# Layer 1's shared second pass moved from behind the expert loop into the routing chain

## The chip, the cores and the metric

The kernel runs on one core of one Trainium2 chip. The core has five engines with their own instruction streams: TensorE (PE: matmuls, transposes), VectorE (DVE), ScalarE (ACT), GpSimd (POOL, which here mostly issues indirect DMAs, "gathers") and SyncE (SP, which here issues DMAs only). They run beside one another and wait for each other by semaphores. The metric is the time of one execution on the device, in microseconds (us). A second, profiled execution gives the trace; its span runs from the first to the last instruction.

## The reference

A "macaron" block on 2048 tokens of 256 numbers: half of a feed-forward layer, an attention-like scan, and half of the same feed-forward layer again, with the same weights.

```python
x = x + 0.5 * ffn(layernorm(x))      # layer 0
x = x + attn(layernorm(x))           # W_in, a scan over the tokens, W_out
x = x + 0.5 * ffn(layernorm(x))      # layer 1, the same weights

def ffn(x):
    scores = sigmoid(gate_w @ x) + gate_b
    weights, indices = top_k(scores, 4)           # 4 of 16 experts
    weights = weights / weights.sum(-1)
    shared_out = silu(x @ w1_shared) * (x @ w3_shared) @ w2_shared    # width 176
    routed_out = sum over the 4 experts e of
        weights[e] * (silu((x @ w1[e]) * (x @ w3[e])) @ w2[e])
    return shared_out + routed_out
```

## The kernel before

The tokens lie in 16 tiles of 128 (NT = 16). They stay in SBUF as `xres` [128 x 16 x 256] from the first load to the last store. Everything is float32, and every engine's stream is written out by hand, with explicit semaphores; nothing reorders it. Loops over experts are hardware loops with a few iterations unrolled.

Each of the two feed-forward layers (f = 0 and f = 1) has the same stages:

1. **Phase A.** Each tile is normalized and written to DRAM (`xn_scratch`, for the gathers). PE turns it, and computes the gate logits and the shared expert's first pass (`hidden`, L1380 with `w_shared`). The silu product, the *shared hidden* rows [128 x 176], stays in SBUF (`hidk`, made of leftover room in `stage`, `raw_shared`, `hid_room` and `ring_f`).
2. **Routing chain.** DVE makes the top-4 masks and weights, PE counts the tokens of each expert (`count`, L1524 and L1526), DVE turns the counts into slots (`route_slots`). Each expert gets whole tiles of 128 slots, 79 in all (NS = 79). PE finds the expert of each slot tile (`tile_experts`, L1533). Then come 16 *picks*, one for each token tile: ACT scales rows (`scale_pick`, L770), and PE multiplies (`pick`, L1540). Out of them comes `tokidx`, the token of each slot (cast at L1095).
3. **Expert loop.** For each of the 79 slot tiles POOL gathers 128 rows (L560), PE turns them (L1402; ACT evicts at L664), and runs the expert's two passes (L1380, L1431). ACT evicts the result, and SP writes it to `ys_scratch` (`y_out`, L449). For the first 8 token tiles the finished expert rows are gathered back and added within the loop ("early" rows).
4. **Behind the loop.** POOL gathers the rows of the other 8 token tiles, 4 each, so 32 gathers (`combine`, L595), and DVE multiplies each with its weight and adds it to `xres` (L1159 in layer 1).

The shared expert's **second pass** (the hidden rows times `w2_shared`) stands in different places in the two layers.

In **layer 0** it runs within the routing chain, in 17 *shared steps*. In step n PE turns the hidden rows of tile n (`turn_early`, L1475: two transposes), ACT copies them to SBUF (`copy_early`, L741), PE multiplies those of tile n-1 (`out_early`, L1488: two matmuls), and ACT evicts the sums of tile n-2 with the factor 0.5 (`evict_early`, L748). Step 0 stands ahead of `count`, steps 1 to 11 between `count` and `tile_experts`, the rest among the picks. Between the steps ACT also turns a few late experts' weights into the format of the matmul (`high_expert`, L645 and L648; `CHAIN_HIGHS` says after which step). SP writes the 16 results to DRAM (`shared_scratch`, L457) and loads them again during the loop, four at a time (`shared_in`, L462). DVE adds each to `xres` in the loop (`shared_rows_first`, L1139).

In **layer 1** SP writes the hidden rows to DRAM (`hid_out`, L453) ahead of the loop, and loads them again (`hid_in`, L467): 6 at the loop's start, 8 more behind the loop's last y_out, 2 after that. The rest is done behind the loop, for 8 pairs of tiles: PE turns a pair (`turn_hidden`, L1506), ACT copies it (`copy_hidden`, L762), PE multiplies (`shared_out`, L1517), and DVE adds the sums to `xres` from PSUM (`shared_sum`, L1181). POOL's 32 gathers are paced by this: ahead of every second gather POOL waits for one more step of PE's work (`SHARED_DONE`). An output tile is stored (L522) once its sum is added; the store of the last tile is the last thing in the kernel.

In the rows, `bank` is PSUM, `mamba_room`, `stage`, `raw_ring`, `ring_f` and `ring_r` are SBUF buffers that serve several purposes, `cst` and `hcst` are constants, and `si` holds the slot numbers for the gathers.

Of the kernel before, what the change touches and what calls it, by code (L numbers as in the profile page):

```python
# [31 lines left out]
LAG_HID = 5  # L32
# [16 lines left out]
HID_AHEAD = 6  # L49
SUMS_AFTER = {9: (0, 1), 10: (2,), 11: (3,), 12: (4,), 13: (5,), 14: (6, 7)}  # L50
CHAIN_HIGHS = {1: (6, 7, 8, 9), 5: (10,), 8: (11,)}
# [34 lines left out]
def build(nc, x_d, w13r_d, w2r_d, w13s_d, w2s_d, wm_d, cst_d, hcst_d, out_d):  # L86
# [7 lines left out]
    with ctx:  # L94
# [9 lines left out]
        hid_dram = nc.dram_tensor("shared_hidden", (N, H), f32, kind="Internal").ap()  # L104
# [44 lines left out]
        hTs = [raw_ring[0:HC, b * 512:(b + 1) * 512] for b in range(4)]  # L149
# [48 lines left out]
        hidb = [r0(b * H, (b + 1) * H) for b in range(HID_AHEAD)]  # L198
        hidb += [mroom[:, 8 * TOPK * D + b * H:8 * TOPK * D + (b + 1) * H] for b in range(8)]
# [14 lines left out]
        p_hS, p_yS = [pb[0], pb[3]], [pb[1], pb[2], pb[4], pb[5]]  # L214
# [24 lines left out]
        s_hw = [sem(f"shared_hidden_written{b}") for b in range(NG)]  # L239
        s_hl = [sem(f"shared_hidden_loaded{b}") for b in range(NT // 2)]  # L240
# [6 lines left out]
        s_st = sem("shared_hidden_turned")  # L247
        s_hs = sem("shared_hidden_copied")
        s_sy = sem("shared_sums")
        s_sa = sem("shared_added")  # L250
# [106 lines left out]
        def steps_in_picks(t):  # L357

            first = SH_ENDS + t * (SH_LAST - SH_ENDS) // NT
            return range(first, SH_ENDS + (t + 1) * (SH_LAST - SH_ENDS) // NT)  # L360
# [60 lines left out]
        def _(sp):  # L421
# [29 lines left out]
            def hid_out(f, t):  # L451
                sp.wait_ge(s_m, f * STEPS + t + 1)
                sp.dma_start(hid_dram[t * P:(t + 1) * P, :], hidk[t]).then_inc(s_hw[t // 4], 16)  # L453

            def shared_out(t):
                sp.wait_ge(s_eo, t + 1)
                sp.dma_start(sh_dram[t * P:(t + 1) * P, :], sh_out[t % 4]).then_inc(s_sw[t % 4], 16)  # L457

            def shared_in(t):
                if t >= 4:  # L460
                    sp.wait_ge(s_sf, t - 3)
                sp.dma_start(shared_rows[t % 4], sh_dram[t * P:(t + 1) * P, :]).then_inc(s_cs[t % 4], 16)  # L462

            def hid_in(t):
                if t >= len(hidb):
                    sp.wait_ge(s_st, (t - len(hidb)) // 2 + 1)
                sp.dma_start(hidb[t % len(hidb)], hid_dram[t * P:(t + 1) * P, :]).then_inc(s_hl[t // 2], 16)  # L467
# [3 lines left out]
            for f in range(2):  # L471
                if f == 1:
                    sp.wait_ge(m_s["res"], NMC)
                for t in range(NT):
                    xn_out(f, t)
                    if f == 1 and t >= LAG_HID:
                        hid_out(f, t - LAG_HID)
                    if f == 0 and t in LATE_AFTER:
                        load_late(MAMBA_E + LATE_AFTER.index(t))
                for e in range(MAMBA_E if f else NE, NE):  # L480
                    load_late(e)
                for t in range(NT - LAG_HID if f else NT, NT):
                    hid_out(f, t)
                for t in range(NT if f == 0 else 0):
                    shared_out(t)
                for k in range(UN if f else 0):
                    y_out(f, 0, k)
                if f == 1:
                    for g in range(NG):
                        sp.wait_ge(s_hw[g], group(0))  # L490
                    sp.wait_ge(s_rt, 2)
                    for t in range(HID_AHEAD):
                        hid_in(t)
                else:
                    sp.wait_ge(s_et, NT)
                    sp.wait_ge(s_rt, 1)
                    for b in range(4):
                        sp.wait_ge(s_sw[b], 16 * (NT // 4))
                    for r in range(NT // 4):
                        for t in range(4 * r, 4 * r + 4):  # L500
                            shared_in(t)
                        for j in range(SHARED_BEHIND[r], SHARED_BEHIND[r + 1]):
                            y_out(0, 0, j)
                    sp.wait_ge(s_sf, NT)
                    sp.dma_start(stage[0][:, 0:1024], wm_d[:, 0:1024]).then_inc(s_wm, 16)
                with sp.Fori(1 if f else SHARED_BEHIND[-1] // UN, NS // UN) as i:
# [7 lines left out]
                for t in range(HID_AHEAD if f else NT, NT):  # L514
                    hid_in(t)
# [11 lines left out]
        def _(pool):  # L527
# [50 lines left out]
            def combine(f, t):  # L578
# [7 lines left out]
                for q in range(TOPK):  # L586
# [45 lines left out]
        def _(act):  # L632
# [103 lines left out]
            def copy_early(n):  # L736

                act.wait_ge(s_et, n + 1)
                if n >= 3:
                    act.wait_ge(s_es, n - 2)  # L740
                act.activation(hTe[n % 3], turned(n)[0:HC, 0:2 * P], ACT.Copy).then_inc(s_eh, 1)  # L741

            def evict_early(t):

                act.wait_ge(s_es, t + 1)
                if t >= 4:
                    act.wait_ge(s_sw[t % 4], 16 * (t // 4))
                act.activation(sh_out[t % 4], p_yE[t % 2][:, 0:D], ACT.Copy, scale=0.5).then_inc(s_eo, 1)  # L748

            def shared_step(n):  # L750

                if n < NT:
                    copy_early(n)
                if n >= 2:
                    evict_early(n - 2)

            def copy_hidden(pair):

                act.wait_ge(s_st, pair + 1)
                if pair >= 4:  # L760
                    act.wait_ge(s_sy, pair - 3)
                act.activation(hTs[pair % 4], p_hS[pair % 2][0:HC, :], ACT.Copy).then_inc(s_hs, 1)  # L762
# [11 lines left out]
            for f in range(2):  # L774
# [27 lines left out]
                if f == 0:  # L802
                    for n in range(SH_BEFORE):
                        shared_step(n)
# [3 lines left out]
                for n in range(SH_BEFORE, SH_ENDS if f == 0 else SH_BEFORE):  # L808
                    for e in CHAIN_HIGHS.get(n, ()):
                        high_expert(f, e)  # L810
                    shared_step(n)
                for e in range(MAMBA_E, NE if f else MAMBA_E):
                    high_expert(f, e)
                for t in range(NT):
# [3 lines left out]
                    for n in steps_in_picks(t) if f == 0 else ():  # L818
                        shared_step(n)
                if f == 0:  # L820
                    for n in range(SH_LAST, NT + 1):
                        shared_step(n)
                    evict_early(NT - 1)
                base += NT
                if f == 1:
                    for g in range(NG):
                        act.wait_ge(s_hw[g], group(0))
                else:
                    for b in range(4):
                        act.wait_ge(s_sw[b], 16 * (NT // 4))  # L830
# [3 lines left out]
                for pair in range(NT // 2 if f else 0):  # L834
                    copy_hidden(pair)
# [81 lines left out]
        def _(dve):  # L917
# [190 lines left out]
            def row_added(f, n):  # L1108
# [5 lines left out]
                elif f == 0:  # L1114
                    dve.wait_ge(s_sf, t + 1)
# [567 lines left out]
```

## Time and profile before

| | us |
|---|---|
| Time, median of 3 runs | 590.1 (585.19 to 593.1) |
| Span of the profiled execution | 644.2 |
| The profiled execution's own time | not listed apart from its span |
| Layer 1: end of `count` on PE | 382.34 |
| Layer 1: expert loop, first to last ACT eviction (L664) | 409.71 to 584.27 |
| Layer 1: first and last gather behind the loop | 593.26, 635.53 |

Over the whole span PE is busy 80%, DVE 67%, ACT 58% and POOL 54%, and the granted TensorE clock is 0.897 on average. The profiled execution is 9% longer than the median of the timed runs; both are of the same program. Times in the rows are microseconds from the span's start, of the profiled execution. An engine's idle time costs nothing unless it lies on the path that ends last.

### The profile page before, as it was taken

The numbers are of one execution on the slowest core, as the hardware profiler recorded it, in microseconds if no ns is written. First come the engines' busy times: TensorE is split into PE (matmuls) and PEld (weight loads), VectorE is DVE, ScalarE is ACT, GpSimd is POOL, SyncE is SP. The second block draws the span as 40 slices with busy tenths as digits, with TensorE's granted clock in tenths as the row PEclk, the third lists the DMA queues.
The fourth block names the chain that finished last, engine by engine and source line by source line (L and its number), as shares of the span: only waits on it lengthen the run. The fifth ranks groups of instructions, "written<-read, shape, count | busy, mean of one in ns | idle before, by whom it ended". The sixth has DMA issues, their size and how long they took to land.

```text
span 644.2 us, 13458 instructions
## 1 busy us (share of the span) xinstructions
PE 517.4 (80%) x3206; PEld 454.5 (71%) x3207; DVE 434.0 (67%) x1459; ACT 376.0 (58%) x1128; POOL 349.6 (54%) x364
## 2 busy tenths in 40 slices
PE   4976799999999999667586943799999899998460
PEld 3954589998888889455465931599988788887350
DVE  6798667767767677527686689467666667666434
ACT  2778466766657567555474664477766666665010
POOL 3899554456556565465311442544565556655764
PEclk9978589999999999697697975599999999999875
DMA  9971245565444445432100560254444454555644
GB/s 297 391 269 68 60 130 156 163 179 153 151 145 135 147 129 138 126 95 79 53 2 0 167 210 0 66 150 133 132 150 131 132 149 130 145 137 142 190 129 121
DMA packets 61149, 88.24 MB, mean 137 GB/s; under 512 B 9499, under 2 KB 46363, under 8 KB 61107
## 3 DMA queue, kind: packets, MB, share of 16 engines
q1 hardware_dynamic: 47379, 50.29, 22.7%
q0 software_dynamic: 13728, 37.50, 22.6%
q8 instruction: 12, 0.20, 0.1%
q14 instruction: 30, 0.25, 0.1%
HBM read 57.22 MB, written 30.54 MB: 136 GB/s over the span
## 4 chain that ended last, share of the span: by engine, by line
PE 56%; DVE 11%; issue 10%; ACT 9%; POOL 5%; another core or an unknown queue 4%; DMA 4%; SPq 1%; ACTq 0%; POOLq 0%; DVEq 0%
PE bank L1380 24%; PE bank L1431 10%; PE bank L1402 6%; POOL mamba_room L595 5%; PE bank L1442 4%; PE bank L1441 4%; PE bank L1599 2%; DMA ys_scratch<-ring_f 2%; PE bank L1488 2%; ACT ring_f L713 1%; ACT ring_r L664 1%; DVE xres L1159 1%; PE bank L1624 1%; PE bank L1453 1%
## 5 line engine op out<-in xcount | busy, mean ns | idle before, releaser
L560 POOL DMA_INDIRECT ring_f<-xn_scratch,tokidx x158 | 149.6, 947 | 153.0 <-PE bank L1402 100.6
L1380 PE MATMUL bank<-w_routed,ring_r 128*128 x948 | 195.5, 342 | 0.9 <-DVE ring_r L954 0.8
L1380 PEld LDWEIGHTS bank<-w_routed,ring_r 128*128 128x128 f32 x948 | 152.2, 192 | 6.6 <-issue 4.1
L1431 PE MATMUL bank<-w_routed,ring_r 128*128 x790 | 119.5, 281 | 3.0 <-ACT ring_f L692 2.1
L1431 PEld LDWEIGHTS bank<-w_routed,ring_r 128*128 128x128 f32 x790 | 110.0, 188 | 4.3 <-issue 4.3
L673 ACT ACTIVATE ring_r<-bank 128x256 fp32r<-128x256 f32 x158 | 60.7, 384 | 71.4 <-PE bank L1442 66.5
L962 DVE TENSOR_TENSOR ring_r<-bank,ring_r 128x128 fp32r<-128x128 f32 x158 | 45.6, 288 | 59.9 <-ACT ring_r L673 47.4
L595 POOL DMA_INDIRECT mamba_room<-ys_scratch,si x64 | 61.6, 962 | 29.1 <-issue 18.4
L954 DVE TENSOR_TENSOR ring_r<-bank,ring_r 128x256 fp32r<-128x256 f32 x158 | 67.1, 425 | 15.1 <-issue 5.4
L1402 PE MATMUL bank<-cst,ring_f 128*128 128x128 f32 x316 | 64.4, 286 | 10.0 <-DMA ring_f<-xn_scratch,tokidx 5.4
L682 ACT ACTIVATE stage<-bank 128x176 f32<-128x176 f32 x158 | 50.6, 320 | 35.7 <-remote 18.2
L664 ACT ACTIVATE ring_r<-bank 128x256 fp32r<-128x256 f32 x158 | 60.3, 382 | 14.5 <-PE bank L1402 10.2
L529 POOL TENSOR_TENSOR w_routed<-raw_routed,w_routed 128x512 fp32r<-128x512 f32 (+1 forms) x38 | 55.3, 1495 | 18.8 <-ACT w_routed L648 18.8
L692 ACT ACTIVATE ring_f<-bank 128x256 f32<-128x256 f32 x158 | 60.3, 382 | 8.0 <-DMA ys_scratch<-ring_f 7.4
L713 ACT ACTIVATE ring_f<-ring_f 128x240 f32<-128x240 f32 x158 | 63.6, 403 | 0.6 <-DVE ring_f L972 0.5
L971 DVE TENSOR_TENSOR ring_f<-bank,stage 128x48 f32<-128x48 f32 x158 | 32.6, 206 | 42.9 <-ACT stage L682 28.8
L1599 PE MATMUL bank<-mamba_room,stage 128*128 128x256 f32 (+1 forms) x144 | 38.7, 420 | 21.0 <-ACT mamba_room L883 18.2
L1441 PE MATMUL bank<-cst,ring_f 128*128 128x128 f32 x158 | 46.0, 291 | 8.8 <-ACT ring_f L713 4.8
L1402 PEld LDWEIGHTS bank<-cst,ring_f 128*128 128x128 f32 x316 | 38.1, 144 | 21.2 <-issue 13.8
L972 DVE TENSOR_TENSOR ring_f<-bank,stage 128x176 f32<-128x176 f32 x158 | 52.3, 331 | 0.0
L1599 PEld LDWEIGHTS bank<-mamba_room,stage 128*128 128x128 f32 x144 | 29.1, 222 | 29.4 <-ACT mamba_room L883 20.5
L964 DVE TENSOR_TENSOR ring_r<-bank,ring_r 64x128 fp32r<-64x128 f32 x158 | 46.5, 294 | 2.1
(172 smaller groups left out, 816.5 us busy)
## 6 DMA issues: line engine op xcount, KB each, us to landing
ys_scratch<-ring_f SPq DMA_DIRECT2D x158, 128.0 KB
raw_routed<-in_w13r SPq DMA_DIRECT2D x6, 704.0 KB, 12.5
xn_scratch<-w_routed SPq DMA_DIRECT2D x32, 128.0 KB, 4.9
raw_routed<-in_w2r SPq DMA_DIRECT2D x6, 512.0 KB, 12.8
raw_routed<-in_w13r SPq DMA_DIRECT2D x8, 352.0 KB, 6.4
ring_f<-xn_scratch,tokidx POOLq DMA_INDIRECT x158
xres<-in_x_in SPq DMA_DIRECT2D x4, 512.0 KB, 6.4
raw_routed<-in_w2r SPq DMA_DIRECT2D x8, 256.0 KB, 6.7
```

The source lines that it names most:

```text
L560: pool.indirect_dma_start(xg[j % UN], None, xn_dram, bass.IndirectOffsetOnAxis(ap=tokidx[:, j:j + 1], axis=0)).then_inc(s_g[j % UN], 16)
L595: pool.indirect_dma_start(room[:, q, :], None, ys_dram[0:tiles_before(t) * P, :], bass.IndirectOffsetOnAxis(ap=si[:, n:n + 1], axis=0)).th ...
L664: act.activation(xT[b][0], p_xT[b][:, 0:DC * P], ACT.Copy).then_inc(s_xhi, 1)
L673: act.activation(hT[b][0], p_hT[b][:, 0:2 * P], ACT.Copy).then_inc(s_hhi, 1)
L692: act.activation(yb[b], p_y[b][:, 0:D], ACT.Copy).then_inc(s_yo, 1)
L713: act.activation(hid[c % 2][:, 0:HD + HB], hid[c % 2][:, 0:HD + HB], ACT.Silu).then_inc(s_s, 1)
L954: dve.tensor_tensor(xT[b][1], p_xT[b][:, 0:DC * P], xT[b][0].bitcast(f32), ALU.subtract).then_inc(s_xlo, 1)
L1380: last = pe.matmul(out, a, b, start=(q == 0), stop=(q == len(terms) - 1))
L1402: last = pe.transpose(p_xT[b][:, q * P:(q + 1) * P], xg[k][:, q * P:(q + 1) * P], ident)
L1431: last = pe.matmul(p_y[b][:, 0:D], a, v, start=(q == 0), stop=(q == 4))
L1441: pe.transpose(p_hT[b][:, 0:P], hid[b][:, 0:P], ident)
L1599: last = pe.matmul(out[:, part(c, e)], m_w[m][:, q * D + e * P:q * D + (e + 1) * P], src[:, part(c, q)], start=(q == 0), stop=(q == DC - 1))
```

## The change

Layer 1 is made like layer 0. Its 17 shared steps run in its routing chain, all between `count` and `tile_experts` but step 0, which stands ahead of `count` (`SH_ENDS` and `SH_LAST` are now a pair, one value for each layer). The weights of experts 12 to 15 are converted between the steps n = 1, 2, 4 and 6. SP writes the 16 results to `shared_scratch` and loads them again in the loop between y_outs; DVE adds them in the loop, whose DVE stream is now unrolled as layer 0's is. The DRAM round trip of the hidden rows (16 stores, 16 loads of 88 KB), and `turn_hidden`, `copy_hidden`, `shared_out` and `shared_sum` behind the loop are gone. POOL's 32 gathers wait for no step of PE's any more. The first 8 output tiles are stored after the early adds, the others after their own adds.

```diff
-SHARED_DONE = [("turned", 1)] + [e for p in range(1, NT // 2) for e in (("turned", p + 1), ("out", p))] + [("out", NT // 2)]
-SH_BEFORE, SH_ENDS, SH_LAST = 1, 12, NT
-SUMS_AFTER = {9: (0, 1), 10: (2,), 11: (3,), 12: (4,), 13: (5,), 14: (6, 7)}
-CHAIN_HIGHS = {1: (6, 7, 8, 9), 5: (10,), 8: (11,)}
+SH_BEFORE, SH_ENDS, SH_LAST = 1, (12, NT + 1), (NT, NT + 1)
+CHAIN_HIGHS = ({1: (6, 7, 8, 9), 5: (10,), 8: (11,)}, {1: (12,), 2: (13,), 4: (14,), 6: (15,)})
...
# SP
-                    if f == 1 and t >= LAG_HID:
-                        hid_out(f, t - LAG_HID)
...
-                for t in range(NT - LAG_HID if f else NT, NT):
-                    hid_out(f, t)
-                for t in range(NT if f == 0 else 0):
-                    shared_out(t)
-                for k in range(UN if f else 0):
-                    y_out(f, 0, k)
...
+                for t in range(NT):
+                    shared_out(f, t)
+                sp.wait_ge(s_et, (f + 1) * NT)
+                sp.wait_ge(s_rt, f + 1)
+                for b in range(4):
+                    sp.wait_ge(s_sw[b], 16 * (f + 1) * (NT // 4))
+                for r in range(NT // 4):
+                    for t in range(4 * r, 4 * r + 4):
+                        shared_in(f, t)
+                    for j in range(SHARED_BEHIND[r], SHARED_BEHIND[r + 1]):
+                        y_out(f, 0, j)
...
             for t in range(NT):
-                sp.wait_ge(s_sa, t // 2 + 1)
-                if t >= EARLY_TILES:
+                if t < EARLY_TILES:
+                    sp.wait_ge(s_ea, EARLY + (t + 1) * TOPK)
+                else:
                     sp.wait_ge(s_cd, combined_to(1, t))
# POOL, combine
-                    if f == 1 and q % 2 == 0 and 2 * k + q // 2 >= 1:
-                        done, pairs = SHARED_DONE[2 * k + q // 2 - 1]
-                        pool.wait_ge(s_st if done == "turned" else s_sy, pairs)
# ACT
-                for n in range(SH_BEFORE, SH_ENDS if f == 0 else SH_BEFORE):
-                    for e in CHAIN_HIGHS.get(n, ()):
+                for n in range(SH_BEFORE, SH_ENDS[f]):
+                    for e in CHAIN_HIGHS[f].get(n, ()):
                         high_expert(f, e)
-                    shared_step(n)
-                for e in range(MAMBA_E, NE if f else MAMBA_E):
-                    high_expert(f, e)
+                    shared_step(f, n)
+                if f == 1:
+                    evict_early(f, NT - 1)
                 for t in range(NT):
                     scale_pick(f, t)
...
-                for pair in range(NT // 2 if f else 0):
-                    copy_hidden(pair)
# DVE
-                    if f or not 0 <= r < NT // 4 or b >= 4:
+                    if not 0 <= r < NT // 4 or b >= 4:
                         return
...
-                for pair in SUMS_AFTER.get(t, ()):
-                    shared_sum(pair)
# PE
                 count(f)
-                for n in range(SH_BEFORE, SH_ENDS if f == 0 else SH_BEFORE):
-                    shared_step(n)
+                for n in range(SH_BEFORE, SH_ENDS[f]):
+                    shared_step(f, n)
                 tile_experts(f)
...
-                if f == 1:
-                    turn_hidden(0)
-                    for pair in range(1, NT // 2):
-                        turn_hidden(pair)
-                        shared_out(pair - 1)
-                    shared_out(NT // 2 - 1)
```

PE's stream at layer 1's routing chain, before: the last of phase A, `count` (two rows), `tile_experts`, the first pick.

```order
L1380 MATMUL bank<-w_shared,ring_r 128x368 x18
L1524 MATMUL bank<-ring_f,hcst 128x256 x4
L1526 MATMUL bank<-ring_f,hcst 128x16x16 x4
L1533 MATMUL bank<-stage,hcst 1x80 x2
L1540 MATMUL bank<-ring_f 128x79 x8
```

The same place in the changed kernel, with its line numbers (turn_early L1405, out_early L1418, `count` L1432 and L1434); the rows left out repeat the pair.

```order
L1310 MATMUL bank<-w_shared,ring_r 128x368 x18
L1405 MATMUL bank<-cst,stage 88x128 x2
L1432 MATMUL bank<-ring_f,hcst 128x256 x4
L1434 MATMUL bank<-ring_f,hcst 128x16x16 x4
L1405 MATMUL bank<-cst,stage 88x128 x2
L1418 MATMUL bank<-raw_shared,raw_ring 128x256 x2
...
L1405 MATMUL bank<-cst,ring_f 88x128 x2
L1418 MATMUL bank<-raw_shared,raw_ring 128x256 x4
L1441 MATMUL bank<-stage,hcst 1x80 x2
L1448 MATMUL bank<-ring_f 128x79 x8
```

Between `count` and `tile_experts`, where nothing stood, there are now 15 turns and 16 products (step 0's turn stands ahead of `count`).

ACT's stream there, in the changed kernel: the last silus of phase A (L684), conversions of late weights (L605, L608), copies of turned rows (L701), evictions (L708), and the first picks (L723). Before, the four pairs of conversions stood in a row, and the picks followed at once.

```order
L701 ACTIVATE raw_ring<-bank 88x256
L594 ACT_TABLE_LOAD
L684 ACTIVATE hid_room<-bank 128x176 x2
L684 ACTIVATE ring_f<-bank 128x176 x2
L605 ACTIVATE w_routed<-raw_routed_55 128x704
L608 ACTIVATE w_routed<-raw_routed_55 128x512
L701 ACTIVATE raw_ring<-bank 88x256
...
L701 ACTIVATE raw_ring<-bank 88x256
L708 ACTIVATE raw_ring<-bank 128x256 x3
L723 ACTIVATE ring_f<-ring_f,cst 128x316 x2
```

Here 16 copies and 16 evictions have come in ahead of ACT's first pick.

SP's queue after the last conversion's loads in layer 1, in the changed kernel: the 16 stores of shared rows, then their loads in four rounds between the y_outs, the rest of the loop, and the outputs.

```order
L438 DMA shared_scratch<-raw_ring 128x256 x16
L443 DMA stage<-shared_scratch 128x256 x4
L434 DMA ys_scratch<-ring_f 128x256 x5
L443 DMA stage<-shared_scratch 128x256 x4
L434 DMA ys_scratch<-ring_f 128x256 x8
L443 DMA stage<-shared_scratch 128x256 x4
L434 DMA ys_scratch<-ring_f 128x256 x8
L443 DMA stage<-shared_scratch 128x256 x4
L434 DMA ys_scratch<-ring_f 128x256 x11
```

Before, 16 stores of hidden rows stood ahead of the first y_out, and the 16 loads stood behind the fourth y_out (6) and behind the loop (10).

## Rows read from the trace of the kernel before

**Rows 1.** Stretches: us, busy of PE, PEld, DVE, ACT, POOL (instructions), clock, DMA share, GB/s.

```profile
411.00:587.00 176.00, 169.38 (x1160) 157.26 (x1160) 120.13 (x412) 117.29 (x384) 98.94 (x105) 0.99 0.48 136
587.00:645.00 58.00, 23.97 (x120) 19.27 (x118) 25.70 (x54) 7.49 (x17) 33.10 (x35) 0.76 0.50 145
```

**Rows 2.** Timeline, POOL behind layer 1's loop: start, us, instruction, idle before and releaser.

```profile
593.26 0.95 POOL L595 DMA_INDIRECT mamba_room<-ys_scratch,si  x1 [0.30 <-issue]
...
612.03 1.12 POOL L595 DMA_INDIRECT mamba_room<-ys_scratch,si  x1 [0.30 <-issue]
616.65 0.94 POOL L595 DMA_INDIRECT mamba_room<-ys_scratch,si  x1 [3.50 <-remote]
...
630.40 1.07 POOL L595 DMA_INDIRECT mamba_room<-ys_scratch,si  x1 [0.30 <-issue]
635.53 0.95 POOL L595 DMA_INDIRECT mamba_room<-ys_scratch,si  x1 [0.30 <-issue]
```

**Rows 3.** Timeline, PE, ACT and DVE behind layer 1's loop.

```profile
600.42 0.60 PE L1506 MATMUL bank<-cst,mamba_room 128*88 128x128 f32 x4
615.89 1.08 ACT L762 ACTIVATE raw_ring<-bank 88x512 f32<-88x512 f32 x2 [14.90 <-remote]
625.70 1.03 PE L1517 MATMUL bank<-raw_shared,raw_ring 88*128 88x256 f32 x4
633.55 0.48 DVE L1159 SCALAR_TENSOR_TENSOR xres<-mamba_room,wk,xres 128x256 f32<-128x256 f32 x1 [0.80 <-DMA mamba_room<-ys_scratch,si]
639.21 0.69 DVE L1181 SCALAR_TENSOR_TENSOR xres<-bank,xres 128x512 f32<-128x512 f32 x1 [4.57 <-remote]
639.93 2.05 DVE L1159 SCALAR_TENSOR_TENSOR xres<-mamba_room,wk,xres 128x256 f32<-128x256 f32 x4
```

**Rows 4.** Timeline, layer 1's routing chain, PE, ACT and DVE.

```profile
380.43 1.91 PE L1526 MATMUL bank<-ring_f,hcst 128*128 128x256 f16 x4
383.28 0.61 ACT L648 ACTIVATE w_routed<-raw_routed 128x512 fp32r<-128x512 f32 x1
394.30 0.29 PE L1533 MATMUL bank<-stage,hcst 128*1 128x80 f16 x2 [11.95 <-DVE si L1068]
395.50 1.16 ACT L770 ACTIVATE ring_f<-ring_f,cst 128x316 f16<-128x316 f16 x2 [11.61 <-DVE ring_f L1082]
405.30 0.24 DVE L1095 CAST tokidx<-bank 128x79 int32<-128x79 f32 x1 [0.97 <-PE bank L1540]
```

**Rows 5.** Timeline, PE, layer 0's shared steps 1, 2, 5, 6, 7 and the product of step 11.

```profile
41.50 0.71 PE L1475 MATMUL bank<-cst,stage 128*88 128x128 f32 x2
...
43.71 0.55 PE L1475 MATMUL bank<-cst,stage 128*88 128x128 f32 x2
...
47.14 0.38 PE L1475 MATMUL bank<-cst,stage 128*88 128x128 f32 x2
...
48.23 0.38 PE L1475 MATMUL bank<-cst,stage 128*88 128x128 f32 x2
...
49.95 0.39 PE L1475 MATMUL bank<-cst,stage 128*88 128x128 f32 x2
...
55.15 1.03 PE L1488 MATMUL bank<-raw_shared,raw_ring 88*128 88x256 f32 x4
```

**Rows 6.** Timeline, ACT's first and last eviction of gathered rows, loops of layers 0 and 1.

```profile
80.94 0.75 ACT L664 ACTIVATE ring_r<-bank 128x256 fp32r<-128x256 f32 x2 [2.19 <-PE bank L1402]
...
254.97 0.38 ACT L664 ACTIVATE ring_r<-bank 128x256 fp32r<-128x256 f32 x1
...
409.71 0.38 ACT L664 ACTIVATE ring_r<-bank 128x256 fp32r<-128x256 f32 x1 [5.09 <-PE bank L1402]
...
584.27 0.38 ACT L664 ACTIVATE ring_r<-bank 128x256 fp32r<-128x256 f32 x1
```

**Rows 7.** Groups by line (count | busy, mean ns | idle): adds; gathers, 81 to 125, 410 to 454.

```profile
L1139 DVE TENSOR_TENSOR xres<-xres,stage 128x256 f32<-128x256 f32 x16 | 6.6, 415 | 0.0
...
L560 POOL DMA_INDIRECT ring_f<-xn_scratch,tokidx x22 | 20.8, 945 | 22.8 <-PE bank L1402 22.5 <-issue 0.3
...
L560 POOL DMA_INDIRECT ring_f<-xn_scratch,tokidx x23 | 21.7, 945 | 22.0 <-PE bank L1402 21.4 <-issue 0.6
```

**Rows 8.** Timeline, SP's queue in layer 0's loop: a round of shared loads.

```profile
99.39 3.40 SPq L462 DMA_DIRECT2D stage<-shared_scratch  x4
```

**Rows 9.** Stretches within the chains of layers 0 and 1, columns as in Rows 1.

```profile
44.00:56.00 12.00, 11.20 (x60) 8.90 (x58) 11.59 (x26) 8.47 (x25) 12.00 (x9) 1.00 0.27 94
379.00:395.00 16.00, 3.03 (x10) 1.28 (x10) 14.66 (x39) 3.93 (x6) 11.24 (x8) 0.50 0.25 89
```

More of the change, by code:

```diff
@@ L148, in build @@
         sh_out = [raw_ring[:, 768 + b * D:768 + (b + 1) * D] for b in range(4)]
-        hTs = [raw_ring[0:HC, b * 512:(b + 1) * 512] for b in range(4)]
         lg = sb("lg", [P, NT, NE])
@@ L355, in turned, with steps_in_picks @@
             return p_hE[2 + n % 2 if n < 4 else n % 4]
-        def steps_in_picks(t):
-            first = SH_ENDS + t * (SH_LAST - SH_ENDS) // NT
-            return range(first, SH_ENDS + (t + 1) * (SH_LAST - SH_ENDS) // NT)
+        def steps_in_picks(f, t):
+            ends, steps = SH_ENDS[f], SH_LAST[f] - SH_ENDS[f]
+            return range(ends + t * steps // NT, ends + (t + 1) * steps // NT)
         def group(f):
@@ L481, in _ @@
                     load_late(e)
-                for t in range(NT - LAG_HID if f else NT, NT):
-                    hid_out(f, t)
-                for t in range(NT if f == 0 else 0):
-                    shared_out(t)
-                for k in range(UN if f else 0):
-                    y_out(f, 0, k)
-                if f == 1:
[L489 to L503, printed above, removed]
+                for t in range(NT):
[9 more added lines that the diff above has]
+                        y_out(f, 0, j)
+                if f == 0:
                     sp.wait_ge(s_sf, NT)
                     sp.dma_start(stage[0][:, 0:1024], wm_d[:, 0:1024]).then_inc(s_wm, 16)
-                with sp.Fori(1 if f else SHARED_BEHIND[-1] // UN, NS // UN) as i:
+                with sp.Fori(SHARED_BEHIND[-1] // UN, NS // UN) as i:
                     for k in range(UN):
@@ L801, in _ @@
                 sigmoid(f, 1)
-                if f == 0:
-                    for n in range(SH_BEFORE):
-                        shared_step(n)
+                for n in range(SH_BEFORE):
+                    shared_step(f, n)
                 table(SET_SILU)
@@ L1259, in _ @@
                 route_slots(f)
-                if f == 1:
-                    for g in range(NG):
-                        dve.wait_ge(s_hw[g], group(0))
-                else:
-                    dve.wait_ge(s_et, 6)
+                dve.wait_ge(s_et, f * NT + 6)
                 for t in range(NT):
@@ L1490, in out_early, with shared_step @@
                 last.then_inc(s_es, 1)
[L1492 removed]
+            def shared_step(f, n):
                 if n < NT:
[L1495 removed]
+                    turn_early(f, n)
                 if n >= 1:
[L1497 to L1519 removed]
+                    out_early(f, n - 1)
             def count(f):
@@ L1554, in _ @@
                         hidden(f, s - 2)
-                for n in range(SH_BEFORE if f == 0 else 0):
-                    shared_step(n)
+                for n in range(SH_BEFORE):
+                    shared_step(f, n)
                 count(f)
-                for n in range(SH_BEFORE, SH_ENDS if f == 0 else SH_BEFORE):
-                    shared_step(n)
+                for n in range(SH_BEFORE, SH_ENDS[f]):
+                    shared_step(f, n)
                 tile_experts(f)
@@ L1562, in _ @@
                     pick(f, t)
-                    for n in steps_in_picks(t) if f == 0 else ():
-                        shared_step(n)
-                if f == 0:
-                    for n in range(SH_LAST, NT + 1):
-                        shared_step(n)
-                    pe.wait_ge(s_eo, NT)
+                    for n in steps_in_picks(f, t):
+                        shared_step(f, n)
+                for n in range(SH_LAST[f], NT + 1):
+                    shared_step(f, n)
+                pe.wait_ge(s_eo, (f + 1) * NT)
                 pe.wait_ge(s_m, base + NT)
```

124 lines of the change are left out of this document (32 added, 92 removed).

## The prediction

> **What bounds the kernel now.** The first view is the busy time by stretches. In layer 1's expert loop PE is busy 169 of 176 us; behind the loop it is busy 24 of 58, and POOL has the largest share, 33.1 us [rows 1]. So the loop is bound by PE, and the stretch behind it by something else; what the move is worth is read at three places, the chain, the loop and the end, and not from the averages.
>
> The second view is the timeline behind the loop. POOL's 32 gathers run one after the other: 0.95 us and 0.30 us between two, a period of 1.25 us [rows 2]. The stream stops once: the 16th starts at 612.03, the 17th at 616.65, after 3.50 us put down to "remote". What the stop waits for has been done for long: PE's turn of a pair ran at 600.42, yet ACT's copy of it starts at 615.89 after 14.90 us of waiting, again for "remote" [rows 3]. In this stretch PE's signals reach the other engines only some time after POOL's stream of gathers has paused. The same shows at the end: the last gather ends at 636.48 (635.53 + 0.95); PE's last product ended at 626.73, but DVE's last two sums wait for it until 639.21, and the last four adds come behind them, 639.93 to 641.98. From there to the end of the span it is 2.22 us, the last store.
>
> The third view is the timeline of layer 1's routing chain. PE ends `count` at 382.34 (380.43 + 1.91) and then does nothing until `tile_experts` at 394.30, for DVE makes slots. ACT ends its conversions at 383.89 and starts the first pick at 395.50, after 11.61 us of waiting for DVE [rows 4]. So 12 us of PE and ACT stand empty there, and the question is whether 16 shared steps fit into them.
>
> **The chain: +7.8 us.** The price of a step is read where the same steps run now, in layer 0: steps 5 and 6 start at 47.14 and 48.23, so 1.09 us for a step; step 7 comes 1.72 us after step 6, since a pair of conversions stands between them on ACT, 0.63 us more; and steps 1 and 2 are 2.21 us apart, at the lower clock. From the start of step 1 (41.50) to the end of step 11's product (56.18) it is 14.68 us, with two such pairs in it [rows 5]. Layer 1 puts all 16 steps ahead of `tile_experts`, and three pairs within them (ahead of steps 2, 4 and 6; the pair ahead of step 1 runs beside `count`). So: 382.34 + 14.68 + 0.63 for the third pair + 4 x 1.09 for steps 12 to 15 + 0.86 for the last product (1.09 less its turn) = 402.9. ACT's last eviction takes some 0.4 us more (an estimate: an ACT instruction of 128x256 takes 0.38 [rows 6]), so its first pick starts at 403.3 in place of 395.50: **+7.8**. DVE's slots are ready at 394.3 as before and hide nothing of that. The picks behind are a pass of ACT and PE of 9.8 us before `tokidx` (395.50 to 405.30), which stays. Bounds: 6 if the clock is high from the first step and the third pair hides; 10 if two more steps run at 2.21.
>
> Costs that hide: the 16 stores of results on SP (the last issued by about 403.5, nothing waits for it before the loop's first y_out); ACT's wait for them ahead of its first eviction, which follows at least 13 us after the first pick (395.50 to 409.71) [rows 4, 6]; DVE's wait for six turned tiles ahead of the picks, passed by step 5 at about 389. The late weights' loads stand no longer behind stores of hidden rows; the conversions they feed ended 11 us early anyway.
>
> **The loop: 0.** It gets 16 adds of 0.415 us on DVE, 6.6 us in all [rows 7], on an engine that is busy 120 of 176 us there [rows 1]; 16 loads on SP between y_outs; and DVE's unrolled stream. All of this stands in layer 0's loop already. From the first to the last eviction that loop takes 174.03 us, layer 1's without all this 174.56 [rows 6]. So nothing. Bounds: -1 (the difference, and a little for DVE's loop branches) to +3.4, one round of loads exposed: four of them held SP's queue for 3.40 us, with y_outs behind [rows 8].
>
> The add reads two SBUF tiles beside POOL's gathers. In layer 0 the 22 gathers of 81 to 125, where half of the adds run, take 945 ns, and the 23 of layer 1 at the same distance into its loop, with no adds, also 945 [rows 7]. The Trainium skill ("SBUF — State Buffer", section "Who interferes with whom") says that a DVE instruction with two SBUF inputs contends with a GpSimd instruction that reads SBUF; by that rule the loop could pay up to the adds' whole 6.6 us. The trace shows no such delay, so the term stays 0.
>
> **Behind the loop: -6.1 us.** All of PE's and ACT's work goes, and with it POOL's waits for it and DVE's sums. The gathers remain, at 1.25 us. The stop of 3.50 becomes the usual 0.30: -3.2, so the last gather ends at 633.28. From the end of a gather to its add it is 2.08 us (630.40 + 1.07 to 633.55 [rows 2, 3]); the last add takes 0.48 and the end 2.22: 638.06 against 644.2, **-6.1**. Of it 2.9 is the end, where two sums and four adds no longer wait for PE's late signal. The first stores of outputs go out during the gathers. Next in line is the gather stream itself, and nothing in the change makes that shorter. Bounds: 0, if the late signals are the profile's alone; -12, if the runs without a profile stop three times instead of once (-9.6) and the end gains 2.4.
>
> **Sum.** +7.8 + 0 - 6.1 = +1.7 on the profiled execution's 644.2 us. That is 9% above the median of the timed runs; scaled by 590.1 / 644.2 = 0.916 the sum is +1.6: **591.7 us**. Two per cent of the median, 11.8 us, is what I take as faster or slower; less than that a measurement of this kernel can hardly tell from no change.
>
> **Rivals.**
>
> *The end gains nothing (chance 0.22).* Then the move only lengthens the chain. For it: the gathers run at 1.25 us whether or not a wait stands ahead of them, and the stop after exactly 16 of them could be POOL's own queue. Against it: ACT's copy waited just as long as the gathers did, for a turn that was done. The time: 590.1 + 0.916 x 7.8 = 597.
>
> *Faster: the paced stream stops often when nobody profiles it (0.12).* The sixteen places where POOL waits for PE are each a chance of a stop of 3.2 us; the profile shows one. With six, the change takes back 19.2 + 2.9, less 7.8: -14.3, so 577. It decides from six stops on (5.6 by the sum). Against it: in the one execution shown, 15 of the 16 waits cost nothing.
>
> *Slower: TensorE stays at the lower clock in the steps (0.10).* Granted clock 1.00 (2.4 GHz) over 44 to 56, where layer 0's steps run; 0.50 (1.2 GHz) in layer 1's chain before, with PE mostly empty [rows 9]. In layer 1 conversions stand ahead of steps 2, 4 and 6, just where layer 0 climbed, so PE has gaps there. If the clock does not rise, each step costs 2.21 instead of 1.09 [rows 5]: 16 x 1.12 = 17.9 more, +19.6 in all and 608. It decides once 10 of the 16 steps run low. Against it: layer 0's steps climbed after two. The Trainium skill ("TensorE: Matmul & The Clock Gate", section "A second HAM failure mode: psum-queue depth-cycling") tells of a kernel that goes round PSUM banks with short idle times between groups of matmuls, whose clock went up and down for it; that is the form of these steps. Layer 0's stretch at 1.00 speaks against it here.
>
> *The loop pays (0.06).* An exposed round of loads or gathers held up: +3 to +6.6, so 594 to 598.
>
> **How the numbers follow.** My forecast has 0.50. The likeliest time is 591.7; its own range, from the bounds of the chain (-1.8, +2.2), the loop (-1, +3.4) and half of the end's, is 586 to 598. The range that should hold the time 8 times in 10 takes in the second and fourth case and the near half of the faster and slower ones: 581 to 602. Faster by over 2% 0.12 (the one case), slower by over 2% 0.10 (the other), within 0.78.
>
> **What would show it.** Right: steps of about 1.09 us behind `count`, ACT's first pick some 21 us after the end of `count` instead of 13.2, a loop of 174 to 175 us between the same evictions, 32 gathers at 1.25 us without a stop, and under 5 us from the last gather's end to the end of the span. Wrong: steps over 2 us, gaps of DVE or ACT in the loop's first third that were not there, a stop among the gathers that no PE signal explains, or a median outside 586 to 598 with those rows as forecast, which would mean that the profiled execution does not stand for the timed ones.

## The result, and the profile after

The changed kernel takes 595.68 us (median of 10 runs, 591.39 to 596.51), the kernel before 590.31 in the same comparison: a ratio of 1.0085, with a 95% interval of 1.0057 to 1.0112, so 5.0 us slower (3.4 to 6.6). The forecast was 591.7, 1.6 us slower; the measured difference lies above that by more than its interval. The sign and the chain's price held; what the end would give back was put three times too high. (That a change of less than 2% can hardly be told from none was wrong too: here 0.85% is told with an interval of 0.3% either way.)

The head of the page of the changed kernel, and under it that of a second profile of the unedited kernel before, taken with the experiments:

```profile
span 594.5 us, 13344 instructions
PE 486.2 (82%) x3206; PEld 447.2 (75%) x3207; DVE 437.0 (74%) x1467; ACT 378.8 (64%) x1152; POOL 352.4 (59%) x364
```

```profile
span 591.3 us, 13458 instructions
PE 494.4 (84%) x3206; PEld 451.9 (76%) x3207; DVE 437.7 (74%) x1459; ACT 374.0 (63%) x1128; POOL 354.2 (60%) x364
```

The second profile of before is 53 us shorter than the first (644.2). Its span fits the timed runs (585.2 to 593.1 us), that of the first does not. So the first was an odd execution, and rows of it that rest on waits don't stand for the timed runs; what made it odd is not shown. I therefore compare the changed kernel with the second.

The timeline of PE in layer 1's chain, changed kernel (`count` L1434, turn_early L1405, out_early L1418, `tile_experts` L1441); rows left out repeat the pair. They answer to [rows 4, 5].

```profile
348.19 1.91 PE L1434 MATMUL bank<-ring_f,hcst 128*128 128x256 f16 x4
349.81 0.72 PE L1405 MATMUL bank<-cst,stage 128*88 128x128 f32 x2
...
352.03 0.62 PE L1405 MATMUL bank<-cst,stage 128*88 128x128 f32 x2
...
353.35 0.38 PE L1405 MATMUL bank<-cst,stage 128*88 128x128 f32 x2
...
354.43 0.39 PE L1405 MATMUL bank<-cst,stage 128*88 128x128 f32 x2
...
355.52 0.38 PE L1405 MATMUL bank<-cst,stage 128*88 128x128 f32 x2
356.30 1.10 PE L1418 MATMUL bank<-raw_shared,raw_ring 88*128 88x256 f32 x4 [0.40 <-ACT raw_ring L708]
357.24 0.38 PE L1405 MATMUL bank<-cst,stage 128*88 128x128 f32 x2
...
367.35 2.10 PE L1418 MATMUL bank<-raw_shared,raw_ring 88*128 88x256 f32 x8
369.38 0.23 PE L1441 MATMUL bank<-stage,hcst 128*1 128x80 f16 x2
```

One step at the lower clock (2.22 us), one in which the clock rises (1.32), then 1.09 us a step, 1.72 where a pair of conversions stands ahead (355.52 to 357.24): the prices of layer 0. ACT in the same stretch, its last eviction and the first pick; then the first pick in the second profile of before:

```profile
369.48 0.38 ACT L708 ACTIVATE raw_ring<-bank 128x256 f32<-128x256 f32 x1 [0.69 <-PE bank L1418]
369.76 1.05 ACT L723 ACTIVATE ring_f<-ring_f,cst 128x316 f16<-128x316 f16 x2
```

```profile
350.65 1.91 PE L1526 MATMUL bank<-ring_f,hcst 128*128 128x256 f16 x4
365.72 1.17 ACT L770 ACTIVATE ring_f<-ring_f,cst 128x316 f16<-128x316 f16 x2 [12.34 <-DVE ring_f L1082]
```

From the last four matmuls of `count` to the first pick it was 365.72 - 350.65 = 15.1 us and is 369.76 - 348.19 = 21.6: **+6.5**. And what the pick waits for has changed. It was DVE. Now ACT goes from its last eviction to the pick without a pause, and DVE, which makes what the picks need, stands idle for 6.07 us until 370.83, waiting for PE's first pick.

The loop, first and last eviction, changed kernel and then before (second profile):

```profile
384.38 0.38 ACT L624 ACTIVATE ring_r<-bank 128x256 fp32r<-128x256 f32 x1 [5.77 <-PE bank L1332]
...
541.66 0.38 ACT L624 ACTIVATE ring_r<-bank 128x256 fp32r<-128x256 f32 x1
```

```profile
379.75 0.38 ACT L664 ACTIVATE ring_r<-bank 128x256 fp32r<-128x256 f32 x1 [4.90 <-PE bank L1402]
...
537.43 0.38 ACT L664 ACTIVATE ring_r<-bank 128x256 fp32r<-128x256 f32 x1
```

157.28 us against 157.68: the adds cost the loop nothing that can be seen here. (My 174 us, [rows 6], were those of the odd execution, in both layers.) Behind the loop, POOL's first and last gather and DVE's last add, changed kernel and then before:

```profile
549.60 0.95 POOL L555 DMA_INDIRECT mamba_room<-ys_scratch,si  x1 [0.30 <-issue]
...
588.62 0.95 POOL L555 DMA_INDIRECT mamba_room<-ys_scratch,si  x1 [0.30 <-issue]
591.46 0.49 DVE L1105 SCALAR_TENSOR_TENSOR xres<-mamba_room,wk,xres 128x256 f32<-128x256 f32 x1 [0.57 <-DMA mamba_room<-ys_scratch,si]
```

```profile
545.36 0.95 POOL L595 DMA_INDIRECT mamba_room<-ys_scratch,si  x1 [0.31 <-issue]
...
585.07 0.95 POOL L595 DMA_INDIRECT mamba_room<-ys_scratch,si  x1 [0.30 <-issue]
588.64 0.48 DVE L1159 SCALAR_TENSOR_TENSOR xres<-mamba_room,wk,xres 128x256 f32<-128x256 f32 x1 [1.18 <-DMA mamba_room<-ys_scratch,si]
```

All 32 gathers of before run without a stop here, and its last add waits for its gather, not for PE. From the first gather to the end of the span it is 45.9 us before (591.3 - 545.36) and 44.9 after: 1.0 us, where the forecast had 6.1.

### The profile page after: what moved, and what is told of

The parts are those of the page before. It is cut to its first block, busy times and chain, and to the rows that moved or that the text cites. A ratio compares the mean times of both kernels' runs of the same rounds, so it can differ in the third digit from the quotient of the medians.

```text
span 594.5 us, 13344 instructions
## 1 busy us (share of the span) xinstructions
PE 486.2 (82%) x3206; PEld 447.2 (75%) x3207; DVE 437.0 (74%) x1467; ACT 378.8 (64%) x1152; POOL 352.4 (59%) x364
## 4 chain that ended last, share of the span: by engine, by line
PE 65%; DVE 9%; ACT 8%; POOL 6%; DMA 6%; issue 6%; POOLq 0%; SPq 0%; ACTq 0%; DVEq 0%
PE bank L1310 29%; PE bank L1361 14%; POOL mamba_room L555 6%; PE bank L1332 6%; PE bank L1418 5%; DMA ys_scratch<-ring_f 3%; PE bank L1371 3%; PE bank L1372 3%; PE bank L1500 1%; PE bank L1405 1%; PE bank L1383 1%; DMA raw_shared<-in_w13s 1%; DVE stage L959 1%; DVE lg L880 1%; DVE xres L1105 1%
## 5 line engine op out<-in xcount | busy, mean ns | idle before, releaser
L908 DVE TENSOR_TENSOR ring_r<-bank,ring_r 128x128 fp32r<-128x128 f32 x158 | 45.9, 290 | 34.9 <-ACT ring_r L633 33.8
L1332 PE MATMUL bank<-cst,ring_f 128*128 128x128 f32 x316 | 62.3, 280 | 6.1 <-DMA ring_f<-xn_scratch,tokidx 6.0
L1105 DVE SCALAR_TENSOR_TENSOR xres<-mamba_room,wk,xres 128x256 f32<-128x256 f32 x64 | 29.0, 481 | 25.2 <-DMA mamba_room<-ys_scratch,si 24.3
L1332 PEld LDWEIGHTS bank<-cst,ring_f 128*128 128x128 f32 x316 | 39.7, 144 | 8.7 <-DMA ring_f<-xn_scratch,tokidx 7.7
L537 POOL DMA_INDIRECT stage<-ys_scratch,si x34 | 33.9, 998 | 20.3 <-issue 8.2
L1310 PE MATMUL bank<-w_shared,ring_r 128*128 128x368 f32 x192 | 41.9, 362 | 3.0 <-DVE ring_r L923 3.0
```

Source lines behind the costliest of these rows:

```text
L1310: last = pe.matmul(out, a, b, start=(q == 0), stop=(q == len(terms) - 1))
L1332: last = pe.transpose(p_xT[b][:, q * P:(q + 1) * P], xg[k][:, q * P:(q + 1) * P], ident)
```

## The experiments

The theory: the steps beyond what fits into DVE's slot-making lengthen the chain, and the end gives back a little. The rivals: the loop pays; the waits behind the loop matter. Ratios are to the kernel before, with their 95% intervals; differences to the changed kernel are taken between ratios, times 590.

**The kernel before again**, unedited, for one profile.

> The kernel before, unedited, for a second profile: the first one's span (644.2 us) is 54 us above its timed runs, that of the changed kernel (594.5) equals its own. If the first profile was an odd execution: a span near 589, both loops near 156 us from first to last eviction of gathered rows instead of 174, no 3.5 us stop among the 32 gathers behind the loop, and no late PE signals. If the profiler slows this kernel as such: a span near 644 again, with the stop and the late signals. The forecast's end term (-6.1) rests on the stop and the late signals, so the first outcome leaves it about -2.9 or less.

Its span is 591.3 (the run itself 593.1); loops of 155.92 and 157.68 us, no stop among the gathers. The row of one ACT instruction, grouped by line, in this profile:

```profile
L682 ACT ACTIVATE stage<-bank 128x176 f32<-128x176 f32 x158 | 50.2, 318 | 7.7 <-PE bank L1380 7.1
```

The same row in the first profile, with 35.7 us of idle time ahead of it:

```profile
L682 ACT ACTIVATE stage<-bank 128x176 f32<-128x176 f32 x158 | 50.6, 320 | 35.7 <-remote 18.2 <-PE bank L1380 11.6 <-issue 3.1
```

So the late signals of PE belong to that one execution. The loss is spread over all of it (of the 52.9 us, 35.0 lie in the two loops, 11.4 between the first loop's last eviction and layer 1's `count`, 6.0 behind the second loop), and was not special to the place where I read it.

**The steps left out.** `shared_step(1, n)` is skipped on PE and ACT, with its stores and waits:

```diff
-                    shared_step(f, n)
-                if f == 1:
-                    evict_early(f, NT - 1)
+                    if f == 0:
+                        shared_step(f, n)
```

> The changed kernel without layer 1's 16 shared steps in the chain (turns, products, copies, evictions and the 16 stores are left out; the loop still loads and adds 16 tiles, those of layer 0): the chain term alone. My forecast's chain term: ACT's first pick 13.2 us after the end of count again instead of about 20, so 6 to 7 us below the changed kernel, about 589. If the loop or the end carries the loss instead, the time stays within 2 us of the changed kernel's 595.7.

589.39 us, ratio 0.9969 (0.9942 to 0.9996): 6.8 us below the changed kernel, some 2 us either way by the two intervals, as forecast. From the end of `count` to the first pick it is the old distance again:

```profile
347.49 1.91 PE L1438 MATMUL bank<-ring_f,hcst 128*128 128x256 f16 x4
362.57 1.17 ACT L725 ACTIVATE ring_f<-ring_f,cst 128x316 f16<-128x316 f16 x2 [13.21 <-DVE ring_f L1029]
```

**The second pass left out of the kernel before.**

```diff
-                    if f == 1 and q % 2 == 0 and 2 * k + q // 2 >= 1:
-                        done, pairs = SHARED_DONE[2 * k + q // 2 - 1]
-                        pool.wait_ge(s_st if done == "turned" else s_sy, pairs)
...
-                for pair in SUMS_AFTER.get(t, ()):
-                    shared_sum(pair)
```

(and `hid_in`, `turn_hidden`, `copy_hidden` and `shared_out` with them)

> The kernel before without the shared second pass behind the loop (turns, copies, products, sums and the loads of hidden rows are left out, and POOL's 16 waits for them; the stores of hidden rows ahead of the loop stay): the end term alone. My forecast: the end is 5.6 us shorter, so about 584.7. If the end gains nothing (the rival with 597): within 1 us of the kernel before, about 590.

588.03 us, ratio 0.9966 (0.9944 to 0.9988): 2.0 us (0.7 to 3.3) is all that the end can give, neither my 5.6 nor nothing. Chain and end add up: +6.8 - 2.0 = +4.8, measured +5.0. (The run also drops the loads of hidden rows within the loop; that the 2.0 us lie behind the loop alone is not shown apart.)

**Steps 12 to 16 among and behind the picks.**

```diff
-SH_BEFORE, SH_ENDS, SH_LAST = 1, (12, NT + 1), (NT, NT + 1)
+SH_BEFORE, SH_ENDS, SH_LAST = 1, (12, 12), (NT, NT)
...
-                if f == 1:
-                    evict_early(f, NT - 1)
...
-                if f == 0:
-                    evict_early(f, NT - 1)
+                evict_early(f, NT - 1)
```

> The changed kernel with layer 1's steps 12 to 15 among the picks and step 16 behind them, as layer 0 has them, in place of all ahead of tile_experts. By the chain term, the first pick comes 5 us earlier and each of the four steps then costs some 0.7 us on ACT among the picks, and the last step about 1: some 1 to 2 us below the changed kernel, 594. If the chain's length does not set the loop's start: the same time as the changed kernel, within 0.5.

594.15 us, ratio 1.0045 (1.0016 to 1.0073), 2.4 us below the changed kernel, though the two intervals overlap. `count`'s last four matmuls and ACT's first pick:

```profile
348.95 1.91 PE L1431 MATMUL bank<-ring_f,hcst 128*128 128x256 f16 x4
364.74 1.06 ACT L723 ACTIVATE ring_f<-ring_f,cst 128x316 f16<-128x316 f16 x2
```

15.8 us, against 15.1 with no steps at all: eleven steps cost 0.7 us, they all but fit. The picks then take 12.5 us to `tokidx` in place of 9.5: 0.7 us for each of the four steps among them. Some place must pay for the last five. And a wait comes in that the changed kernel does not have: the last shared row is now made behind the picks, and ACT may begin the loop only when all shared rows are stored. ACT's last eviction of such a row, and its first of the loop:

```profile
379.31 0.38 ACT L708 ACTIVATE raw_ring<-bank 128x256 f32<-128x256 f32 x1 [0.68 <-PE bank L1415]
382.81 0.67 ACT L624 ACTIVATE ring_r<-bank 128x256 fp32r<-128x256 f32 x2 [3.12 <-DMA shared_scratch<-raw_ring]
```

It is 5.59 us from `tokidx` (377.22) to this first eviction, against 5.09 in the changed kernel, and here it waits for the store.

**The first loads held back.**

```diff
+                    if f == 1 and r == 0:
+                        sp.wait_ge(s_xt, STEPS + NT + 4)
                     for t in range(4 * r, 4 * r + 4):
                         shared_in(f, t)
```

> The changed kernel, where SP issues layer 1's first four loads of shared rows only after PE has turned four gathered tiles. Seen: from tokidx to the first eviction of the loop it takes 5.09 us in the changed kernel, 4.22 in the second profile of the kernel before, 4.32 without the second pass; in the first the four loads are issued 0.07 us ahead of the first gather, which lands 3.7 us after its issue instead of 2.8. If the loads delay the gather: first eviction 4.2 to 4.4 us after tokidx, the kernel 0.8 us shorter, about 594.9. If the steps' clock or the stores do it: still 5 us, and 595.7.

The place behaves as the first reading in the expectation says. In the changed kernel four loads go out just ahead of the first gather, and PE's first transpose comes 3.69 us after that gather's issue:

```profile
379.73 1.75 SPq L443 DMA_DIRECT2D stage<-shared_scratch  x4
379.80 0.99 POOL L523 DMA_INDIRECT ring_f<-xn_scratch,tokidx  x1 [18.32 <-DVE tokidx L1041]
383.49 0.69 PE L1332 MATMUL bank<-cst,ring_f 128*128 128x128 f32 x2 [4.31 <-DMA ring_f<-xn_scratch,tokidx]
```

With the loads held back it is 2.89:

```profile
380.10 0.99 POOL L525 DMA_INDIRECT ring_f<-xn_scratch,tokidx  x1 [18.30 <-DVE tokidx L1043]
382.99 0.69 PE L1334 MATMUL bank<-cst,ring_f 128*128 128x128 f32 x2 [3.50 <-DMA ring_f<-xn_scratch,tokidx]
```

From `tokidx` to the first eviction it is 4.28 us instead of 5.09. The time doesn't tell: 595.89 us, ratio 1.0075 (1.0050 to 1.0101), against 1.0085. The 0.8 us at this place is shown; that it reaches the end is not.

**The loop's loads and adds left out.**

```diff
-                        shared_in(f, t)
+                        if f == 0:
+                            shared_in(f, t)
...
-                    if not 0 <= r < NT // 4 or b >= 4:
+                    if f or not 0 <= r < NT // 4 or b >= 4:
```

> The changed kernel without the 16 loads of shared rows and the 16 adds in layer 1's loop (left out; the steps and their stores stay): the loop's term alone. My forecast put it at 0: the loop stays 157 us, and with the loads away from its start the kernel is about 0.8 us shorter, 594.9. If the adds or the loads cost the loop something (bound +3.4): 592 to 594.

594.72 us, ratio 1.0061 (1.0032 to 1.0090): 1.4 us below the changed kernel, and the intervals overlap. 0.8 us of it would be the loop's start (4.25 us from `tokidx` here too), and the loop is 156.06 us from first to last eviction, but other runs' loops differ by as much (155.2 to 158.2). So no more than a microsecond or so shows as the loop's.

**The waits alone taken from the kernel before** (the three lines of `SHARED_DONE` on POOL).

> The kernel before with POOL's 16 waits for PE's steps behind the loop taken out, and nothing else. In its second profile the 32 gathers run without a stop, so by that profile the waits cost nothing: the time of the kernel before, within 1 us. If stops like the 3.5 us of the first profile are common in timed runs: 2 to 4 us shorter, 587 to 589.

591.92 us, ratio 1.0005 (0.9981 to 1.0029). The waits of the gathers for PE's steps cost nothing that this run can tell (1.1 us at most, by the interval). This is also the evidence of timed runs against my rival by which the stream stops often.

**Spread steps and held-back loads together.**

> The changed kernel with steps 12 to 16 among and behind the picks (as run before: 594.15, a ratio of 1.0045 to the kernel before) and with the first four loads held back until PE has turned four tiles. If the two parts add: 0.8 us less, a ratio of 1.003, some 593 against the kernel before's 591. The chain still pays about 4 us and the end gives back about 2, so I expect no gain over the kernel before.

594.08 us, ratio 1.0031 (1.0006 to 1.0056): not below the kernel before, as expected. The 0.8 us isn't seen at its place, though: 5.60 us from `tokidx` to the first eviction. The first transpose comes 3.16 us after the gather's issue and is done by 384.23, yet ACT's first eviction starts at 385.72. Its last eviction of shared rows, behind the picks, starts at 382.21, 3.51 us earlier. In the run with spread steps alone the same distance is 3.50 us, and the row there names the wait, the store of the shared rows; so in these two runs the store sets the loop's start, and holding back the loads can bring nothing. That part of my expectation was wrong.

**A cheaper product.** In layer 1 the steps' products are in fp32r, and a slice of `w_shared` stands in the place of `w2_shared`. A step has two recorded matmuls for its product where it had four:

```diff
-                    last = pe.matmul(p_yE[t % 2][:, 0:D], hTe[t % 3][:, q * P:(q + 1) * P],
-                                     w2_shared[:, q * D:(q + 1) * D], start=(q == 0), stop=(q == 1))
+                    last = pe.matmul(p_yE[t % 2][:, 0:D], hT1[:, q * P:(q + 1) * P],
+                                     w2[:, q * D:(q + 1) * D], start=(q == 0), stop=(q == 1))
```

(`hT1` is a part of `ring_r`, typed fp32r, to which ACT's copy now goes; `w2` is that slice of `w_shared`)

> The changed kernel with layer 1's 32 products of the steps (88x128 by 88x256) in the one-pass format fp32r and with the shared expert's first-pass weights in place of w2_shared, so a wrong factor; instructions, copies and evictions stay in number and place. In the changed kernel a step is 1.09 us, of which PE's two float32 products take 0.86 and its turn 0.22; ACT's copy and eviction take 0.27 each. If PE's products set the step's price: steps of 0.55 to 0.75 us (ACT or the turn bounds them), all 16 fit the 12 us of slot-making, the first pick comes 14 to 15 us after count instead of 20.6, and the time is that of the run without steps, about 589.4. If the price is the round trip between PE and ACT: steps stay near 1 us, the pick at 19 to 20, and 594 to 596.

594.95 us, ratio 1.0046 (1.0013 to 1.0080): 2.3 us below the changed kernel, not 6, and the intervals overlap. The steps are cheaper, but not by half, and the stretches by window say most of why (us, then busy of PE, PEld, DVE, ACT and POOL, the clock, DMA share, GB/s), first of this run, then of the changed kernel:

```profile
348.00:366.00 18.00, 16.36 (x67) 12.32 (x65) 15.12 (x41) 12.77 (x36) 10.19 (x7) 0.57 0.27 95
```

```profile
350.00:356.00 6.00, 5.90 (x27) 4.60 (x25) 5.62 (x12) 4.46 (x11) 3.22 (x3) 0.79 0.12 44
356.00:370.00 14.00, 13.30 (x70) 10.59 (x70) 8.45 (x22) 9.21 (x28) 5.48 (x4) 1.00 0.35 122
```

The clock stays at 1.2 GHz through most of the steps (0.57 over the 18 us), where with the float32 products it rises within the second. PE's timeline shows the moment at which it rises, products (L1421) and turns (L1406):

```profile
362.12 0.77 PE L1421 MATMUL bank<-w_shared,ring_r 88*128 88x256 f32 x2
362.69 0.63 PE L1406 MATMUL bank<-cst,hid_room 128*88 128x128 f32 x2
363.30 0.48 PE L1421 MATMUL bank<-w_shared,ring_r 88*128 88x256 f32 x2
363.62 0.38 PE L1406 MATMUL bank<-cst,ring_f 128*88 128x128 f32 x2
```

A pair of products takes 0.77 us until then and 0.48 in the last four steps, a turn 0.63 and then 0.38. The 16 steps take 16.6 us (349.58 to 366.15, the start of the first and the end of the last) instead of 19.6 (the 20.6 in the expectation counts from the last recorded matmul of `count`, 0.9 us before its group ends; by the same count it is 17.5 here). The clock is not all of it. In the last steps without conversions a step takes 0.98 us at the lower clock (turns starting from 357.78 to 362.69, five steps) and 0.79 at the higher one (products starting from 363.30 to 365.68, three steps). By these figures the clock costs some 2 us over the 12 low steps (an estimate), and PE also stood idle for 0.59, 0.23 and 0.29 us in the early steps, where ACT had conversions to do.

My slower rival had this form: conversions on ACT leave gaps on PE, and the clock stays low. In the changed kernel PE was busy for 4.00 of the 4 us from 349 to 353, in which the clock rose; here for 6.17 of the 7 us from 349 to 356, at 0.50. Whether it was the gaps or the shorter products that kept the clock low, no run separates.

No run points to a version that beats the kernel before. Without any second pass behind the loop that kernel is 2.0 us faster, so this is the most that any other place for it can bring, and the places tried cost more. A split (eleven steps in the chain, the rest behind the loop) could keep part of the 2.0 us; it was not tried, since a part of it lies within the intervals above.

## Why the prediction came out so

- **What bounds the kernel: partly.** The chain was read rightly: 12 us of PE and ACT stood empty, and eleven steps fit into them but for 0.7 us. The stop among the gathers and PE's late signals [rows 2, 3] were those of one odd execution.
- **The chain, +7.8 forecast: right.** +6.5 in the profile, 6.8 in timed runs, inside the bounds 6 to 10. The three pairs of conversions did not each cost 0.63: one did (355.52 to 357.24), the next made its step 0.10 longer (1.19 us from 358.33), and the first lay beside a step at the lower clock.
- **The loop, 0: held**, within a microsecond or so. The gathers' 945 ns beside the adds [rows 7] were no accident: with adds in both loops the 158 gathers of the changed kernel take 948 ns on average, with adds in one they took 947 and 950 in the two profiles of before. The contention that I bounded at the adds' whole 6.6 us does not show in these rows. The Trainium skill ("SBUF — State Buffer", section "Who interferes with whom") reports a probe in which `tensor_copy` seemed to stall DMA and `tensor_tensor` did not; the adds here are of the second kind, and the trace agrees. What I missed is a place, not a size: the first four loads meet the loop's first gather, 0.8 us.
- **Behind the loop, -6.1: wrong, the step that failed.** Measured -2.0 (0.7 to 3.3). "-3.2" for the stop and nearly all of "2.9 is the end" were priced from rows that timed runs don't have. The bound for it was there ("0, if the late signals are the profile's alone"), and I took -6.1 all the same. In its place the runs show a stream that does not stop and an end that waits for its own last gather: without the waits the kernel takes the same time (ratio 1.0005), and without the whole second pass it is 2.0 us faster. The span of 644.2 against runs of 585 to 593 was the sign, and I scaled it away with 0.916 instead of asking which stalls it was made of.
- **The time.** 595.7 lies in the range 586 to 598 because the range is wide; the likeliest value was 4.0 us too low, nearly all of it from the end. (By its own terms the range should have ended at 599.6: 591.7 + 0.916 x (2.2 + 3.4 + half of 6.1).)
- **The rivals.** "The end gains nothing" (0.22, 597) was nearer to the time, 595.7, than my forecast, since no stop was there to win back and the gathers ran at their own pace; but the end did gain 2.0 us. Its other reason, a stop that is POOL's own after 16 gathers, fell with the second profile of before, where no stop comes. "The paced stream stops often" is refuted by the run without the waits. "The clock stays low" did not happen in the change: 1.00 over 356 to 370. Of the signs that I named, the steps' price (1.09 us), the first pick (19.7 us after the end of `count`, forecast some 21), the gathers without a stop and the 4.9 us from the last gather's end to the end of the span came as forecast; the loop's 174 us did not. The last two that came say little: before, by its second profile, the gathers had no stop either, and its end took 5.3 us.

## What to carry to other kernels

Work moved into a gap was nearly free up to the gap's length (0.7 us for eleven steps) and cost its full price beyond it: count the steps that fit, here eleven of sixteen, before moving all. Work behind a loop beside a stream that sets the end (here 32 gathers at 1.25 us) can be nearly free already, and taking it away brings only what the stream's end still waits for. And where the profiled execution is longer than the timed runs, find out first whether its stalls occur in them; a wait put down to "remote" whose producer had long finished was no price here.

## What the runs showed of the hardware

- One profiled execution of the same program took 644.2 us and another 591.3, with the same instructions. In the long one ACT stood idle for 35.7 us ahead of the 158 copies of one kind in the loops (L682), half of it put down to "remote", in place of 7.7 us, while a matmul of the loops took as long in both (342 and 340 ns for L1380). The cause is open.
- A cheaper product went with a slower TensorE. With fp32r products, which kept it busy for 16.36 of 18 us in shorter matmuls and with gaps of 0.2 to 0.6 us between some, the granted clock was 0.57, against 0.79 and then 1.00 with float32 products; of the 6 us that the steps were to save, 3.0 came.
- Four loads of 128 KB issued 0.07 us ahead of a gather put off its arrival by 0.8 us (3.69 us from issue to PE's first use of it, against 2.89 with the loads held back).
